# Top-2 choices read straight from PSUM, row means from x, routing weights on GpSimd and a new order of the drain in an attention and mixture-of-experts kernel

## The reference

```python
# x (4,512,512), ctx (4,512,128), Wg (8,512), W1, W2 (8,352,512), W3 (8,512,352)
p   = layernorm(x)                            # rows of 512
kv  = ctx @ W_k.T + b_k
out = einsum('bij,bjd->bid', p, kv)
sim = einsum('bid,bjd->bij', out, kv) * 512**-0.5
sim = (sim - mean(sim)) * rsqrt(var(sim) + 1e-6) * ln_gamma + ln_beta
x   = x + softmax(sim)                        # the attention matrix itself is added
n   = layernorm(x)
s, i = top_k(n @ Wg.T, 2)                     # 8 experts, 2 for each row
w   = softmax(s)
x   = x + sum over the 2 experts e of  w_e * (silu(n @ W1[e].T) * (n @ W2[e].T)) @ W3[e].T
```

## Time and profile before

| | us |
|---|---|
| median of 3 runs (lowest, highest) | 397.23 (396.95, 398.83) |
| the profiled execution: its time | 397.77 |
| the profiled execution: its span | 395.9 |
| TensorE busy | 366.6 (93%) |
| VectorE busy | 250.1 (63%) |
| ScalarE busy | 230.0 (58%) |
| GpSimd busy | 159.7 (40%) |
| mean granted clock of TensorE | 0.946 |

### The profile page before, as it was taken

The page is one execution under the profiler, slowest core; times in us unless marked ns, Lnnn a source line. Parts: engine busy times, 40 slices in busy tenths (PEclk is TensorE's granted clock), DMA queues, the critical chain, the costliest instruction groups (busy, mean ns, idle before and its releaser), DMA issues.

```text
span 395.9 us, 8248 instructions
## 1 busy us (share of the span) xinstructions
PE 366.6 (93%) x2364; PEld 245.2 (62%) x2364; DVE 250.1 (63%) x665; ACT 230.0 (58%) x402; POOL 159.7 (40%) x188
## 2 busy tenths in 40 slices
PE   6889998987799799999999999999999999999981
PEld 5555766665796456566666666666666666666640
DVE  1366868888346885753476767667676766767660
ACT  1155846544340798984576666756666675666650
POOL 2127663555623214225534353433435344343421
PEclk9999998986657899999999999999999999999997
DMA  7999999767680214425353544535354453535423
GB/s 228 403 407 334 340 410 327 247 230 269 218 294 7 78 29 75 84 57 96 65 105 60 106 67 95 81 83 93 73 105 67 95 83 79 101 65 105 68 41 53
DMA packets 22121, 57.61 MB, mean 146 GB/s; under 512 B 4864, under 2 KB 4992, under 8 KB 20544
## 3 DMA queue, kind: packets, MB, share of 16 engines
q0 software_dynamic: 8736, 20.53, 28.8%
q1 hardware_dynamic: 11184, 20.17, 14.5%
q10 hardware_dynamic: 2160, 16.38, 11.4%
HBM read 38.17 MB, written 18.91 MB: 144 GB/s over the span
## 4 chain that ended last, share of the span: by engine, by line
PE 68%; issue 12%; POOL 9%; DVE 4%; DMA 3%; ACT 2%; POOLq 1%; ACTq 0%; DVEq 0%
PE bank L1281 35%; PE bank L1302 15%; PE bank L1292 5%; PE bank L1272 4%; PE bank L1324 3%; POOL rstd L426 2%; POOL vr L423 2%; PE bank L1123 2%; PE bank L1047 1%; POOL alpha L417 1%; DMA out<-kvj_s,sidx 1%; DMA ng_s<-n_table,gidx 1%; POOL n_s L429 1%; ACT L_s L560 1%; PE bank L1144 1%
## 5 line engine op out<-in xcount | busy, mean ns | idle before, releaser
L1281 PE MATMUL bank<-Wp,kvg_s 128*128 x480 | 79.2, 315 | 1.5 <-DVE kvg_s L990 1.3
L1281 PE MATMUL bank<-Wp,kv_s 128*128 x456 | 74.3, 313 | 0.2
L984 DVE SCALAR_TENSOR_TENSOR stage<-W,w3sc,stage 128x512 f16<-128x512 f16 x93 | 66.8, 746 | 7.1 <-ACT stage L652 7.1
L1302 PE MATMUL bank<-stage,n_s 128*128 128x512 f16 (+1 forms) x279 | 65.3, 379 | 1.5 <-issue 1.5
L1281 PEld LDWEIGHTS bank<-Wp,kvg_s 128*128 128x128 f16 x480 | 47.1, 98 | 29.9 <-issue 5.0
L652 ACT ACTIVATE stage<-W,w3sc 128x512 f16 x93 | 63.2, 717 | 0.0
L517 POOL DMA_INDIRECT out<-oT_s,sidx x20 | 31.8, 1592 | 76.3 <-ACT oT_s L683 69.0
L1281 PEld LDWEIGHTS bank<-Wp,kv_s 128*128 128x128 f16 x456 | 44.4, 98 | 26.5 <-issue 3.4
L517 POOL DMA_INDIRECT out<-kvj_s,sidx x19 | 30.1, 1584 | 66.6 <-ACT kvj_s L683 64.0
L1011 DVE TENSOR_TENSOR n_s<-bank,n_s 128x384 f16<-128x384 f32 x31 | 17.3, 558 | 51.7 <-ACT n_s L665 51.7
L501 POOL DMA_INDIRECT ng_s<-n_table,gidx x39 | 38.9, 997 | 24.7 <-issue 11.3
(11 more groups left out here) (198 smaller groups left out, 560.5 us busy)
## 6 DMA issues: line engine op xcount, KB each, us to landing
Wp<-in_w ACTq DMA_DIRECT2D x7, 1408.0 KB, 8.5
W<-in_w ACTq DMA_DIRECT2D x8, 768.0 KB, 5.7
W<-in_x SPq DMA_DIRECT2D x12, 256.0 KB, 9.8
out<-W SPq DMA_DIRECT2D x12, 256.0 KB, 5.7
stage<-in_xT SPq DMA_DIRECT2D x2, 1024.0 KB, 7.5
Wp<-in_xT SPq DMA_DIRECT2D x2, 1024.0 KB, 9.1
n_table<-n_s SPq DMA_DIRECT2D x8, 256.0 KB, 4.8
n_table<-x_s SPq DMA_DIRECT2D x8, 256.0 KB, 7.3
```

Source lines behind the costliest of these rows:

```text
L984: eng.scalar_tensor_tensor(w3p[r][:, W3N + c * D:W3N + (c + 1) * D], W3[:, bass.ds(e * W3N + c * D, D)], w3sc[:, bass.ds(e, 1)], w3p[r][:, ...
L1281: mm = eng.matmul(bank[2 * which + r][:, 0:H], n_, w_, start=(c == 0 and k == 0), stop=(c == DC - 1 and k == 2))
L1302: mm = eng.matmul(ybank(t)[:, :], h_, w_, start=(c == 0 and k == 0), stop=(c == HC - 1 and k == 2))
```

## The change

Eight things move. (1) `choices` reads the scores from PSUM; the copy to `sc` is gone and the next router waits for `s_ti`, the indices. (2) `xneg` is now minus the mean of the old x minus 1/512, since each softmax row sums to one; it is made in `scale_in`, `new_row` accumulates nothing and no longer waits for the squares and norm of the group before. (3) The routing weights of batches 0 and 1 go to GpSimd's slot i = 2, after its norm, and their store to SyncE's slot i = 3. (4) `gram_copy` goes to ScalarE, ahead of `o_evac`. (5) `diagonal` stands ahead of L867. (6) `mean_square` and `scale_in` for i = 3 stand ahead of the choices. (7) The squared weight norms go to bank 1, behind the router. (8) On TensorE `turn_n` stands ahead of `table(0)` and `table(1)` in slot 15, and the drain has a new order, with 3 x 12 warm matmuls fewer in slots 17 to 19 and 12 more in slot 20.

```diff
# GpSimd, slot
+                if i == 2 and real(b - 2) and b < B:
+                    router_weights(b - 2)
# SyncE, slot
-                if i == 1 and real(b - 2):
+                if real(b - 2) and i == (3 if b < B else 1):
                     router_store(b - 2)
# ScalarE
+            def gram_copy(b):
+                eng.wait_ge(s_Gp, b + 1)
+                wait(eng, s_ogp, b)
+                eng.activation(G_s[:, :], bank[0][:, 0:C], ACT.Copy, scale=1.0 / N).then_inc(s_G, 1)
...
                 eng.wait_ge(s_xn, g + 1)
+                eng.wait_ge(s_x1, g + 1)
...
                 if i == 2 and real(b + 1):
+                    gram_copy(b + 1)
                     o_evac(b + 1)
# VectorE, scale_in
+                wait(eng, s_sq, g - 3)
+                wait(eng, s_n, g - 3)
+                eng.tensor_scalar(xneg[:, g % 4:g % 4 + 1], mv[:, k, 0:1], -1.0, -1.0 / D, ALU.mult, ALU.add).then_inc(s_xn, 1)
# VectorE, new_row
-                wait(eng, s_sq, g - 1)
-                wait(eng, s_n, g - 1)
-                eng.scalar_tensor_tensor(x_s[g], L_s[:, k, :], einv[:, k:k + 1], x_s[g], ALU.mult, ALU.add,
-                                         accum_out=xsum[:, k:k + 1]).then_inc(s_x1, 1)
-                eng.wait_ge(s_x1, g + 1)
-                eng.tensor_scalar(xneg[:, k:k + 1], xsum[:, k:k + 1], -1.0 / D, None, ALU.mult).then_inc(s_xn, 1)
+                eng.scalar_tensor_tensor(x_s[g], L_s[:, k, :], einv[:, k:k + 1], x_s[g], ALU.mult, ALU.add).then_inc(s_x1, 1)
# VectorE, choices
-                if g > G - TPB:
-                    scores = score_bank(g)[:, 0:E]
-                else:
-                    scores = sc[:, :]
-                    eng.tensor_copy(scores, score_bank(g)[:, 0:E]).then_inc(s_sc, 1)
-                    hold(eng, 5, (s_sc, g + 2))
+                scores = score_bank(g)[:, 0:E]
# VectorE, slot
+                n = TPB * (b + 1) + i - (TPB - 1)
+                for k in range(E):
+                    if n == GRAM_SLOTS[k][-1] + 1:
+                        diagonal(k)
                 if real(b):
...
-                if i == 2 and real(b + 1):
-                    gram_copy(b + 1)
-                if i == 0 and real(b - 2) and b < B:
-                    router_weights(b - 2)
+                if i == TPB - 1 and real(bn_):
+                    mean_square(bn_)
+                    scale_in(bn_, in_)
                 b3, i3 = lag(b, i, 4)
...
-                if i == TPB - 1 and real(bn_):
-                    mean_square(bn_)
-                    scale_in(bn_, in_)
# TensorE, router
-                    eng.wait_ge(s_sc, g + 1)
+                    eng.wait_ge(s_ti, g + 1)
# TensorE, drain
                 if n == 17:
-                    eng.wait_ge(s_wmax, 1)
                     router(B - 1, 0)
-                    rank(2)
-                    warm(ones16[:, :], WARM_SLOT)
                     turn_n(B - 1, 2)
                     router(B - 1, 1)
                 if n == 18:
-                    warm(ones16[:, :], WARM_SLOT)
                     turn_n(B - 1, 3)
+                    rank(2)
                     router(B - 1, 2)
                 if n == 19:
-                    warm(ones16[:, :], WARM_SLOT)
                     router(B - 1, 3)
                 if n == 20:
                     warm(ones16[:, :], WARM_SLOT)
                     counts()
                     rank(3)
                     table(2)
-                    warm(ones16[:, :], 2 * WARM_SLOT)
+                    warm(ones16[:, :], 3 * WARM_SLOT)
                     table(3)
# TensorE, slot: weight_norms(n) behind router; counts() waits for s_wmax instead of s_msq
-                if n == 15:
-                    eng.wait_ge(s_wq, E)
-                    table(0)
-                    table(1)
                 if n > GRAM_SLOTS[E - 1][-1]:
+                    if n == 2 * E - 1:
+                        eng.wait_ge(s_wq, E)
                     warm(ones16[:, :], WARM_SLOT)
...
                 turn_n(*lag(b, i, 2))
+                if n == 15:
+                    eng.wait_ge(s_wq, E)
+                    table(0)
+                    table(1)
```

More of the change, by code:

```diff
@@ L160, in build @@
         einv = sb("einv", [P, 2])
-        xsum = sb("xsum", [P, 2])
-        xneg = sb("xneg", [P, 2])
+        xneg = sb("xneg", [P, 4])
         ssq = sb("ssq", [P, 2])
@@ L165, in build @@
         rstd = sb("rstd", [P, 2])
-        sc = sb("sc", [P, E])
         top = sb("top", [P, TPB, 8])
@@ L252, in build @@
             sem(n) for n in ("s_bn", "s_mv", "s_va", "s_al", "s_S", "s_T", "s_L", "s_E", "s_ei", "s_x1")]
[L253 to L254 removed]
+        s_xn, s_sq, s_vr, s_rs, s_n, s_nTp, s_nT, s_scp, s_top, s_ti = [
+            sem(n) for n in ("s_xn", "s_sq", "s_vr", "s_rs", "s_n", "s_nTp", "s_nT", "s_scp", "s_top", "s_ti")]
         s_r = sem("s_r")
@@ L428, in norm @@
                 hold(eng, 0, (s_rs, g + 1), (s_stn[g % 4], 16 * (g // 4)), (s_nTp, g - 3))
-                eng.tensor_scalar(n_t[g % 4], x_s[g], xneg[:, k:k + 1], rstd[:, k:k + 1], ALU.add, ALU.mult).then_inc(s_n, 1)
+                eng.tensor_scalar(n_t[g % 4], x_s[g], xneg[:, g % 4:g % 4 + 1], rstd[:, k:k + 1], ALU.add, ALU.mult).then_inc(s_n, 1)
             def weight_scale():
@@ L636, in _ @@
             kvj_evac(0)
+            gram_copy(0)
             o_evac(0)
@@ L704, in centre_keys @@
                 eng.tensor_scalar(kv_s[:, :], kv_s[:, :], kneg[:, 0:1], None, ALU.add).then_inc(s_kvc, 1)
-            def gram_copy(b):
-                eng.wait_ge(s_Gp, b + 1)
-                wait(eng, s_ogp, b)
-                eng.tensor_scalar(G_s[:, :], bank[0][:, 0:C], 1.0 / N, None, ALU.mult).then_inc(s_G, 1)
             def square_in(b):
@@ L724, in x_stats @@
                 eng.bn_stats(bn[:, k, :], x_s[g]).then_inc(s_bn, 1)
-                hold(eng, 3, (s_bn, g + 1))
+                hold(eng, 3, (s_bn, g + 1), (s_xn, g - 1))
                 eng.bn_aggr(mv[:, k, :], bn[:, k, :]).then_inc(s_mv, 1)
@@ L834, in choices @@
                 eng.wait_ge(s_ti, g + 1)
-                if g > G - TPB:
-                    scores = score_bank(g)[:, 0:E]
-                else:
-                    scores = sc[:, :]
-                    eng.tensor_copy(scores, score_bank(g)[:, 0:E]).then_inc(s_sc, 1)
-                    hold(eng, 5, (s_sc, g + 2))
+                if i == 0:
+                    wait(eng, s_dl, b)
+                    wait(eng, s_wi, b)
+                scores = score_bank(g)[:, 0:E]
                 eng.max(top[:, i, :], scores).then_inc(s_top, 1)
@@ L868, in slot @@
                                              lmin[:, k:k + 1]).then_inc(s_L, 1)
-                n = TPB * (b + 1) + i - (TPB - 1)
-                for k in range(E):
-                    if n == GRAM_SLOTS[k][-1] + 1:
-                        diagonal(k)
                 if i == 0 and real(b + 1) and b >= 0:
@@ L924, in _ @@
             eng.tensor_scalar(beta_s[:, :], beta_s[:, :], -1.0, None, ALU.mult).then_inc(s_ngam, 1)
-            gram_copy(0)
             batches(slot)
@@ L1155, in weight_norms @@
             def weight_norms(n):
-                wait(eng, s_sc, n - 4)
+                eng.wait_ge(s_msq, B)
                 eng.wait_ge(s_wq, E)
-                eng.matmul(bank[7][:, E:2 * E], ones[:, :], wsq[:, :], start=True, stop=True).then_inc(s_wqp, 1)
+                eng.matmul(bank[1][:, E:2 * E], ones[:, :], wsq[:, :], start=True, stop=True).then_inc(s_wqp, 1)
             def weight_gram(k, first, last):
```

24 lines of the change are left out of this document (5 added, 19 removed).

## The result

The changed kernel takes 392.28 us (median of 4 runs, 391.79 to 392.99) where the kernel before takes 397.58 (4 runs, 396.95 to 398.83): ratio 0.9864, 95% interval 0.9833 to 0.9895. The forecast of 390.2 lies 2.1 us under it, inside its range of 386.5 to 395.5; as a ratio to the 397.23 it started from it was 0.982, just outside the interval. The gain is clear of the noise and about three quarters of what was forecast (5.3 us of 7.0). The profiled execution took 392.64, with a span of 390.9 against 395.9.

What follows compares the result with a forecast made beforehand. TensorE bounds experts and batches, so gains come only as an earlier first gather, through VectorE's chain and the low-clock drain. 1.4 + 3.8 + 3.1 - 1.3 = 7.0 us off 397.77 gives 390.8, said as 390.2; range 386.5 to 395.5.

Steps and rivals of the forecast that it cites:

- The drain: First router to `counts`: three warm blocks go, 3.7 us, less a loss; net 3.1 us gained, bounds 2.0 and 6.
- the loss of 0.6: In the drain, `columns(2)` between the last two choices makes the last choices late, partly hidden by warm matmuls: 0.6 us lost.
- the tables of batch 3 before 93 us: Sign to be seen: the table of batch 3 starts before 93 us, against 94.37 in the old profile.
- 1.7 with a bound of 2.2: Batch 3 up to the tables: VectorE sheds 1.8 us together, 1.7 taken for the tables' start, bounds 0.8 and 2.2.
- the start of batch 2: Earlier `va` ends GpSimd's 1.12 us idle and cuts TensorE's 1.64 us wait: 1.4 us gained, bounds 0.5 and 2.05.
- I count nothing: Start of batch 1: GpSimd is full up to alpha there, so no gain or loss is counted.
- `msq` comes only after the choices: Start of batch 2: reason given why GpSimd's alpha stood 1.12 us for VectorE's `va`.
- the price is at most 0.4 … and I take 0.1: Opening of batch 3: GpSimd's routing weights, some 1.5 us ahead of alpha, mostly fit in slack; 0.1 us lost.
- GpSimd becomes the bound: Rival, chance 0.2: norms end as before, counts 1.4 us later, batch 3 opens 0.5 to 1 late; 393.3 us.
- the likeliest case: The main forecast of 390.2 us, chance 0.5, with its own range of 388.5 to 392.5.
- the same 8.26 us of work … no longer interrupted: Batch 3's tables to the drain's first router: TensorE's work stays 8.26 us, its 2.09 us wait goes; 2.1 us gained.
- the last warm block: Before the last table: 12 more warm matmuls at 0.106 us each cost 1.3 us, bounds +0.0 and +1.3.

Runs made afterwards that it cites:

- e13: Changed kernel with the copy of the scores to SBUF back for groups 0 to 12, the next router waiting for it: 393.72 us, ratio 0.9866.
- e1: Changed kernel with all eight diagonals back behind the minimum: 392.46 us, ratio 0.9841 to the kernel before.
- e2: Changed kernel with only the first diagonal (slot 2) back behind the minimum: 392.39 us, ratio 0.9847 to the kernel before.
- e12: Changed kernel with the first diagonal back behind the minimum, and `mean_square` and `scale_in` for i = 3 back behind the choices: 391.95 us, ratio 0.983.
- e3: Changed kernel with the routing weights of batches 0 and 1 back on VectorE and their store back in SyncE's slot i = 1: 392.12 us, ratio 0.9857.
- e8: Changed kernel with 24 warm matmuls before the last table instead of 36: 390.93 us, ratio 0.9839 to the kernel before.
- e9: Changed kernel with 18 more warm matmuls in each of TensorE's two gaps of batch 3: 391.72 us, ratio 0.9842.
- e5: Changed kernel with TensorE's old drain: old order, three warm blocks in slots 17 to 19, 24 warm matmuls before the last table: 395.24 us, ratio 0.9925.
- e10: Changed kernel with first diagonal behind the minimum, routing weights of batches 0 and 1 on VectorE, 24 warm matmuls before the last table: 391.01 us, ratio 0.9819.

## Why the forecast was right, and where 1.9 us went

**Right.** The drain: 3.09 us where 3.1 were forecast, and 10.45 us from first router to `counts` where 10.4 were. The mechanism was there too: the three blocks of 1.24 us are gone without any idle in their place but 0.30 us, and the loss of 0.6 that was set against them is seen too: the last MAX8 starts only as VectorE's `columns(2)` end, at 111.53, and `counts` comes 1.73 us behind the start of its warm block instead of 1.25. Of what was to be seen these came: VectorE's 3.65 us gone, no wait for the weight sums, the nT copy with no wait, no norm waited for in the drain (the last ends at 103.50, forecast 103.7), experts untouched. These did not: the tables of batch 3 before 93 us (94.34, with a warm block and the turn now ahead of them) and the gather near 119.6 (121.65). `gram_copy` on ScalarE and the store on SyncE hold up nothing that the rows show, though SyncE's store waits for GpSimd and a store of x is queued behind it (81.01 and 81.43 us); no run has them alone. From the first minimum of batch 3 to the last diagonal VectorE needs 7.77 us instead of 9.87: 2.10 shed, where I had taken 1.7 with a bound of 2.2. Three reads of PSUM for one copy cost nothing (e13). The Trainium skill (VectorE: DVE Perf Modes, Rules for kernel authors) advises the copy where many operations follow; for these tiles of 128x8 the trace does not bear that out.

**Right in sum, wrong in parts: the start of batch 2.** -1.39 us as forecast, but out of +0.87 and -2.26. "I count nothing" for the start of batch 1 was wrong: the diagonal ahead of the minimum is the change's fifth part, I priced it only where the weight grams were long done, and in slot 2 it waits for TensorE (e1, e2). The gain itself was larger than its bound of 2.05: 0.95 of wait, and 1.31 in the instructions behind it at the full clock, of which I had taken a third of 0.93. And the reason given, "`msq` comes only after the choices", is not what counted (e12): `va` came early enough without the new order.

**Wrong: "the price is at most 0.4 … and I take 0.1".** This is GpSimd's routing weights, and the costliest step up to the last diagonal that failed. They take 2.01 us (78.95 to 80.96), not 1.5, and push `alpha` of batch 3 by 1.06 us (e3). I had set them against a slack of GpSimd read in the trace of before: the idle ahead of `alpha` while it waited for `va`. But the change itself makes `va` earlier, and with that the slack is gone (e3 has no idle ahead of `alpha` either); every operation ahead of `alpha` is then on the path. Batch 3 opens 0.21 us earlier, not 1.4. The rival "GpSimd becomes the bound" had just this ("batch 3 opens 0.5 to 1 late") together with late norms in the drain, which did not come; its 391.5 to 395 holds the result, and the likeliest case's 388.5 to 392.5 holds it barely.

**Wrong: "the same 8.26 us of work … no longer interrupted".** The wait of 2.09 us is gone, but the work took 9.89 us. The 8.26 had been done at a mean clock of 0.66, the 9.89 at 0.50. I carried busy time over from a stretch whose clock was partly up as if the clock were a property of the work. The gap of 1.12 us that GpSimd made ends 2.4 us ahead of the fall (1.00 up to 87.0 us, 0.50 from 87.2); that it is the cause is not shown, since e8 has the same gap and its clock was back at 1.00 from 89.5 to 92.9. With the gaps filled it is still 8.64 (e9), so of the 1.63 us some 1.25 hang on the clock of this execution and 0.38 stay. From the last diagonal to the router the gain was 0.46, where 2.1 were forecast. It is partly luck of the execution: e5 and e8, with the same code up to there, need 10.26 and 9.23 us, the changed kernel 10.24; before it was 10.70, and the forecast took 2.1 off. The Trainium skill (TensorE: Matmul & The Clock Gate, What's actually happening) says that activity releases the throttle; this trace gives 24 us with hardly a gap in TensorE's rows, 92 to 116 (23.47 us busy), all at 0.50, so busy rows alone don't tell that the level will rise.

**Luck: the last warm block.** +1.3 us forecast, +0.73 measured (e8: 0.72). 36 matmuls took 3.44 us, where at 0.50 throughout they take 4.02 (e1 and e9); here the clock came back at 117.8 us, in the last of them. Six of nine traces with the 36 pay 1.2 to 1.4, so the forecast's size was sound and this execution came off cheaply. What was wrong is that the table itself would be shorter at full clock: the last one took 2.03 us at 1.00, and 2.05 at 0.50 before.

In sum, from the forecast 7.0: less 1.19 for the opening of batch 3, plus 0.40 for VectorE in it, less 1.64 around the tables, less 0.01 in the drain, plus 0.57 for the last warm block, makes 5.13, which is the gather's gain. From there to the end 0.05 is gained and 0.18 was lost ahead of the first turn of keys: 5.0 us of span.

**Open.** That the dropped wait for the norm, with the shorter work behind it, is what freed `va` is argued, not tried alone. The order of the drain and its warm blocks were not tried apart. Why the clock stays at 0.50 through the drain is not known; e9 shows only that it isn't the gaps before it.

## What to carry to other kernels

Slack read in the old trace is spent by whatever the same change makes earlier: when an operation moves to another engine, recompute who comes last at that point with the change's own new times. Moving an operation ahead of another needs its inputs checked in every slot, the first one too. And filler matmuls that keep a clock up are worth a trial without them wherever the profile shows the low level in spite of them: here the drain without its three blocks of twelve, in its new order, was worth 3 us, two blocks fewer ahead of it 1.4, and the one that the change had added cost 0.7 to 1.4. Read the price of a stretch from more than one execution where its clock moves: the same code took 9.2 or 10.3 us here.

## What the hardware showed that I had not expected

- The table matmuls cost the same at either level: 16 of them 3.89 us at 1.00 (e9) and 3.92 at 0.50, with 3.5 us of weight loads beside them in e9's trace. In e9 and e10 the clock fell within 0.8 us behind them; in e10 it had risen while they ran.
- A long stretch of small matmuls with almost no idle in the rows can stay at the lower level: 24 us here, and a router's 8 matmuls take about 1.7 us there and 0.96 at full.
- GpSimd's short operations stretch beside VectorE's. The same 128x1 operation took 0.34 or 0.85 us, the 128x512 one 0.77 or 1.31, and `wden` 0.63 at 78.95 and 0.20 in the drain. In the changed kernel's trace from 40 to 116 us `vr` took 0.77 to 0.90 us all six times that VectorE had a large operation on two SBUF tiles beside it (the minimum, the new x or a 128x1024 one), and 0.34 all seven times that it had none. The Trainium skill (GPSIMD Engine Reference, Specifications) says that GpSimd shares its SBUF interfaces with VectorE, with contention where VectorE's instruction has two SBUF inputs; these rows agree and give the size.
